# ScalarE takes the input and candidate gates of the next group's first cell ahead of the cell tanh that ends the present group

## The chip, the cores and the metric

One core of one Trainium2 chip runs the whole program. The metric is the device time of the core in microseconds (us), the median of three runs. All data is float32.

## The reference

Four graph layers run one after the other on `x` of shape (32 batches, 256 nodes, 128 features), each with a residual sum and a layer norm behind it. The change lies in the last layer, an LSTM over windows of nodes:

```
for p in range(1, 5):
    nw = 256 // p
    wins = h[:, :nw*p].reshape(B*nw, p, 128)
    # LSTM over the p nodes of each window, zero initial state
    #   i, f, g, o = split(x_t @ Wih.T + h @ Whh.T + bias)
    #   c = sigmoid(f)*c + sigmoid(i)*tanh(g)
    #   h = sigmoid(o)*tanh(c)
    h[:, every p-th node] = last hidden state
x = layernorm(x + h)
```

The first three layers are a gated graph convolution, a graph convolution with batch norms, and graph attention.

## The kernel before

The batches are worked in 8 groups of 4 (`GROUPS`, `GB`). After the first two layers, which run as stages of their own, a software pipeline of slots s = 2 to 10 handles groups at different depths (`slots`): slot s does the attention of group s (flag A, while s < 8), the graph part of the LSTM layer for group s-1 (B), the LSTM cells of group s-2 (L), and the transposes, last norm and output of group s-3 (T). So a slot lasts about as long as the eleven LSTM cells of one group, and the cells of the next group begin where the slot ends.

`STEPS` lists the eleven cells of a group, k = 0 to 10: k = 0 and 1 are the two halves of the p = 1 window (512 columns each, no previous state, so gates I, G, O alone), k = 2 and 3 are p = 2 (512 columns), k = 4 to 6 are p = 3 (340 columns), k = 7 to 10 are p = 4 (256 columns). A cell goes over three engines:

- TensorE: `lstm_x` (L831) multiplies the gate weights with the input into one PSUM bank per gate (`Q[q]`, shown as QQ); `lstm_h` (L843) adds the part with the previous hidden state. One float32 matmul shows as two rows of the trace.
- ScalarE: `lstm_gates` takes the tanh of each gate out of PSUM (L1200, into `TG`, shown as raw). Then `lstm_state` takes the tanh of the cell state (L1236, from `CELL` into `TC`, both shown as raw).
- VectorE: `lstm_cell` (L1680, L1686, L1690) forms `CA = (1+I)*G`, `CF = (1+F)*CELL` and `CELL`; for a first cell one L1680 gives `CELL`. `lstm_state` (L1708) forms the hidden state from `TG[O]` and `TC`, into `HT` or `HS` (shown as HB).

Below, x(k) and h(k) are the two matmul sets of cell k, I(k), G(k), F(k), O(k) its gate tanhs, CELL(k) the VectorE instruction that writes the cell state, TC(k) the tanh of it, and H(k) VectorE's hidden state. Cell 0 after a cell 10 belongs to the next group.

The orders on the engines are written out by hand; each engine runs its own list in order, and semaphores tie the lists together. Around the end of a slot:

- TensorE: h(10) of the present group, the last matmuls of the attention, x(0) of the next group, the transposes of the residual (`a_residual`, L680, only where flag A holds), x(1), the transposes of the group before (`t_turn`, L884), a graph product (`a_spread0`, L786), x(2). x(0) waits only until each bank is read by cell 10's gate tanh; x(1) until it is read by cell 0's. `t_turn` waits for the H(10) of the group that it turns, and x(2) for H(1):

```
            def t_turn(g, par):
                pe.wait_ge(h_ok, NSTEP * (g + 1))
...
                elif s == 0 and p > 1:
                    pe.wait_ge(h_ok, NSTEP * g + LAST_BEFORE[p] + 1)
```

- VectorE: CA(10), CF(10), CELL(10), H(10), the statistics of a norm (`a_stats2`, L1400, where A holds), CELL(0), a residual sum (L1552, where A holds), H(0), CELL(1), six short norm instructions (L1412 to L1422), H(1).
- ScalarE: the gates of cell 10, TC(10), the gates of cell 0, TC(0), the gates of cell 1, TC(1).

In the last two groups (`HALVED`) the cell tanh and the hidden state are made in two halves (L1234 with L1236, L1705 with L1708, VectorE's cells in L1722 to L1738). In the last slot with cells (s = 9) the group is alone: TensorE runs x(0), `t_turn`, x(1), and from k = 2 on the cells run in two lanes (L1219, L865). There `t_turn` turns group 6, whose H(10) ends slot 8.

Of the kernel before, what the change touches and what calls it, by code (L numbers as in the profile page):

```python
# [46 lines left out]
I, F, G, O = range(4)  # L47


def gates_of(k):  # L50

    return [I, G, O] if STEPS[k][1] == 0 else [I, G, F, O]
# [48 lines left out]
def build(nc, x, xt, adj, early_in, later_in, lstm_w, out):  # L101
    ctx = ExitStack()
    with ctx:
# [6 lines left out]
        def reach(eng, s, n):  # L110

            if isinstance(n, int) and n <= 0:
                return
            eng.wait_ge(s, n)
# [182 lines left out]
        def middle(k):  # L297
            return STEPS[k][3] // 2 * GB
# [736 lines left out]
        def _(act):  # L1035

            def norm_apply(k, kk, z, g, to, h=None):
                act.wait_ge(ln[k]["off"], halves(g, h) if k == 1 else g + 1)
                for b in batches(h):
                    for c in range(NC):  # L1040
                        t = 2 * b + c if k == 1 else c * GB + b
                        act.activation(nth(to, t), nth(z, t), ACT.Identity, bias=OFF[kk][:, t:t + 1],  # L1042
                                       scale=RSD[kk][:, t:t + 1]).then_inc(ln[k]["out"], 1)
# [100 lines left out]
            def a_lin(g, some):  # L1144
                f = front(g)
                for b in some:
                    act.wait_ge(wh_ok, 2 * g + b // 2 + 1) if g < 2 else act.wait_ge(s12_ok, g - 1)
                    act.wait_ge(max_ok, TILES * g + 2 * b + 2)
                    reach(act, et_ps, GB * before(g))
                    for c in range(NC):  # L1150
                        t = 2 * b + c
                        s1 = f.WH[:, t, P:P + 1] if g < 2 else S12[:, 0, t:t + 1]
                        e = act.activation(f.E1[:, t], f.MS[:, t], ACT.Prelu, bias=s1, scale=1.0, alpha=SLOPE)
                    e.then_inc(lin_ok, 1)

            def a_exps(g, some):
                f = front(g)
                for b in some:
                    act.wait_ge(eb_ok, 2 * g + b // 2 + 1)
                    act.wait_ge(lin_ok, GB * g + b + 1)  # L1160
                    for c in range(NC):
                        t = 2 * b + c
                        e = act.activation(f.E1[:, t], f.E1[:, t], ACT.Exp, bias=f.EB[:, t:t + 1], scale=1.0,  # L1163
                                           accum_out=DEN[:, t:t + 1] if g > 1 else None)
                    e.then_inc(exps_ok, 1)

            def a_spread(g, h=None):
                act.wait_ge(sp_ps, halves(g, h))
                reach(act, y0_ps, 2 * g)
                act.activation(S0T[:, part(h)], PA[:, part(h)], ACT.Copy).then_inc(sp_ok, size(h))  # L1170

            def a_relu(g, h=None):
                act.wait_ge(y0_ok, halves(g, h))
                act.activation(H0T[:, part(h)], H0T[:, part(h)], ACT.Relu).then_inc(h0_ok, size(h))
# [4 lines left out]
                act.activation(by_batch(HT[:, par])[:, 2 * h:2 * h + 2], PA[:, part(h)].rearrange("p (b n) -> p b n", n=NODES),  # L1179
                               ACT.Relu, scale=2.0).then_inc(h1_ok, 1)  # L1180

            def lstm_gates(g, k):
                p, s, _, nw = STEPS[k]
                n = nw * GB
                j = NSTEP * g + k
                for q in gates_of(k):
                    act.wait_ge(g_ps, NGATE * g + GATE_AT[k, q] + 1)

                    if q == O:
                        reach(act, h_ok, j)  # L1190
                    elif q == F or STEPS[k - 1][1] > 0:
                        reach(act, cf_ok if q == F else ca_ok, FORGETS[NSTEP] * g + FORGETS[k])
                    else:
                        reach(act, cell_ok, j)
                    at = 0
                    if q == F and (g >= HALVED or k == HALF_STEP):
                        at = middle(k)
                        act.activation(TG[q][:, 0:at], Q[q][:, 0:at], ACT.Tanh, scale=0.25,
                                       bias=BL[:, p - 1, q:q + 1]).then_inc(f_half, 1)
                    act.activation(TG[q][:, at:n], Q[q][:, at:n], ACT.Tanh, scale=0.5 if q == G else 0.25,  # L1200
                                   bias=BL[:, p - 1, q:q + 1]).then_inc(g_ok, 1)

            def lane_gates(k, l, some=None):
                p, s, _, nw = STEPS[k]
                v, c = lanes[l], lane_cols(k, l)

                if s == 0 and l == 1 and k > LANED:
                    act.wait_ge(lanes[0].h, lanes[0].step0 + k - LANED)
                for q in some or gates_of(k):
                    act.wait_ge(v.ps, lane_gate(l, k, q))  # L1210
                    if k == LANED:
                        act.wait_ge(h_ok if q == O else cell_ok, NSTEP * LAST + LANED)
                    elif q == O:
                        act.wait_ge(v.h, v.step0 + k - LANED)
                    elif q == F or STEPS[k - 1][1] > 0:
                        reach(act, v.cf if q == F else v.ca, v.forget0 + FORGETS[k])
                    else:
                        act.wait_ge(v.cell, v.step0 + k - LANED)
                    act.activation(TG[q][:, c], v.banks[q][:, c], ACT.Tanh, scale=0.5 if q == G else 0.25,  # L1219
                                   bias=BL[:, p - 1, q:q + 1]).then_inc(v.ok, 1)  # L1220

            def lane_state(k, l):
                v, c = lanes[l], lane_cols(k, l)
                act.wait_ge(v.cell, v.step0 + k - LANED + 1)
                act.activation(TC[:, c], CELL[:, c], ACT.Tanh, scale=0.5).then_inc(v.tc, 1)

            def lstm_state(g, k):
                n = STEPS[k][3] * GB
                j = NSTEP * g + k
                at = 0  # L1230
                if g >= HALVED or k == HALF_STEP:
                    at = middle(k)
                    act.wait_ge(cell_half, halved(g, k)[0])
                    act.activation(TC[:, 0:at], CELL[:, 0:at], ACT.Tanh, scale=0.5).then_inc(tc_half, 1)  # L1234
                act.wait_ge(cell_ok, j + 1)
                act.activation(TC[:, at:n], CELL[:, at:n], ACT.Tanh, scale=0.5).then_inc(tc_ok, 1)  # L1236

            def slot(s, par, A, B, L, T):
                def gates(k):
                    lstm_gates(s - 2, k) if L else None  # L1240

                def state(k):
                    lstm_state(s - 2, k) if L else None

                def cell(k):
                    gates(k)
                    state(k)

                cell(0)
                cell(1)  # L1250
                if s == LAST + 2:
                    for k in range(LANED, NSTEP):

                        first, last = STEPS[k][1] == 0 and k > LANED, k + 1 < NSTEP and STEPS[k + 1][1] == 0
                        lane_gates(k, 0, (O,) if first else None)
                        lane_state(k, 0)
                        lane_gates(k, 1)
                        lane_gates(k + 1, 0, (I, G)) if last else None
                        lane_state(k, 1)
                    return  # L1260
                cell(2)
                a_spread(s - 1, None if A else 0) if B else None
                norm_apply(1, 0, Z, s, X2) if A else None
                cell(3)
                a_spread(s - 1, 1) if B and not A else None
                cell(4)
                a_lin(s, (0,)) if A else None
                gates(5)
                a_relu(s - 1) if B else None
                state(5)  # L1270
                if A:
                    a_lin(s, (1,))
                    a_exps(s, (0,))
                    a_lin(s, (2,))
                gates(6)
                a_lin(s, (3,)) if A else None
                state(6)
                a_exps(s, (1, 2)) if A else None
                gates(7)
                a_exps(s, (3,)) if A else None  # L1280
                state(7)
                cell(8)
                a_mixed(s, (0, 1, 2)) if A else None
                cell(9)
                a_mixed(s, (3,)) if A else None
                cell(10)

            act.wait_ge(bn_ok, HC + 1)
            act.wait_ge(out2_ok, 2 * GROUPS)
# [664 lines left out]
```

## Time and profile before

| | us |
|---|---|
| median of 3 runs | 638.23 |
| lowest, highest | 637.72, 639.11 |
| span of the profiled execution, first to last instruction | 636.4 |
| TensorE matmul rows busy | 621.6 (98%) |
| VectorE busy | 474.8 (75%) |
| ScalarE busy | 433.8 (68%) |
| GpSimd busy | 167.4 (26%) |

The span is what the trace covers; it is 1.8 us below the median of the timed runs, and the profiled execution has no other time. A busy share is an average over stages. Matmuls overlap in the rows: consecutive ones start closer together than one lasts, so whether TensorE is held up is read from the distance of starts, not from the busy share alone. PEld rows are its weight loads.

### The profile page before, as it was taken

Reading aid. Unit: us, or ns where it says so; the run is one execution under the profiler, and the core shown is the slowest. Engines: PE = TensorE matmul, PEld = TensorE weight load, DVE = VectorE, ACT = ScalarE, POOL = GpSimd, SP = SyncE. Lnnn points to the kernel's source line nnn. Section 1 sums busy time; section 2 is a strip of 40 time slices with the busy share of each in tenths; the row PEclk is TensorE's granted clock in tenths of the full one; section 3 lists DMA queues with packets and bytes.
Section 4 is the critical chain, followed back from the end, with each engine's and each line's share of the span. In section 5 each row is a group of like instructions: output and inputs, shape, how many; then the busy total and the mean of one; then the engine's idle time right before and its main releaser. Section 6 shows DMA issues by size and latency. Waiting matters only on the chain.

```text
span 636.4 us, 9580 instructions
## 1 busy us (share of the span) xinstructions
PE 621.6 (98%) x2768; PEld 440.9 (69%) x2768; DVE 474.8 (75%) x1623; ACT 433.8 (68%) x995; POOL 167.4 (26%) x228
## 2 busy tenths in 40 slices
PE   9999999999999999999999999999999999999994
PEld 6756656447975687578658757865885687577794
DVE  4999999876847767866887787688768767465656
ACT  3667767966947766795677577557847766546774
POOL 1464551005233002304503240341143032103211
PEclk9999999999999999999999999999999999999998
DMA  8424000000000000000000000000000000000000
GB/s 337 142 115 166 1 1 1 1 0 2 2 1 1 0 2 0 2 2 33 2 0 2 34 1 2 33 2 1 1 33 2 2 28 6 1 1 33 2 35 33
DMA packets 4372, 16.84 MB, mean 26 GB/s; under 512 B 480, under 2 KB 480, under 8 KB 4192
## 3 DMA queue, kind: packets, MB, share of 16 engines
q1 hardware_dynamic: 4320, 16.23, 6.6%
q8 instruction: 22, 0.36, 0.2%
q14 instruction: 30, 0.25, 0.1%
HBM read 12.03 MB, written 4.19 MB: 26 GB/s over the span
## 4 chain that ended last, share of the span: by engine, by line
PE 76%; DVE 3%; ACT 2%; issue 1%; POOL 0%; POOLq 0%; ACTq 0%; DVEq 0%
PE QQ L831 26%; PE QQ L843 15%; PE PA L814 4%; PE PA L786 4%; PE PB L805 2%; PE PB L796 2%; PE PB L667 2%; PE PA L667 2%; PE PA L767 2%; PE PB L767 2%; PE QQ L865 1%; PE PB L884 1%; PE PB L746 1%; PE PA L746 1%; PE QQ L875 1%
## 5 line engine op out<-in xcount | busy, mean ns | idle before, releaser
L1200 ACT ACTIVATE raw<-QQ,BL 128x256 f32<-128x256 f32 (+2 forms) x279 | 150.1, 558 | 75.1 <-PE QQ L843 37.7
L831 PE MATMUL QQ<-HT,WT 128*128 128x256 f32 (+2 forms) x558 | 183.9, 474 | 1.1 <-ACT raw L1200 0.6
L446 POOL TENSOR_TENSOR RSD<-VAR,pw 128x4 f32<-128x4 f32 (+1 forms) x43 | 61.8, 1438 | 381.7 <-DVE VAR L1422 381.7
L831 PEld LDWEIGHTS QQ<-HT,WT 128*128 128x128 f32 x558 | 103.5, 190 | 59.2 <-issue 28.3
L843 PE MATMUL QQ<-HB,WT 128*128 128x256 f32 (+2 forms) x336 | 100.2, 441 | 0.4 <-DVE HB L1708 0.2
L843 PEld LDWEIGHTS QQ<-HB,WT 128*128 128x128 f32 x336 | 61.2, 190 | 29.3 <-issue 13.4
L1236 ACT ACTIVATE raw<-raw 128x256 f32<-128x256 f32 (+4 forms) x79 | 37.1, 470 | 25.9 <-DVE raw L1690 19.7
L1680 DVE SCALAR_TENSOR_TENSOR raw<-raw 128x256 f32<-128x256 f32 (+2 forms) x60 | 32.5, 542 | 20.2 <-ACT raw L1200 19.6
L1708 DVE SCALAR_TENSOR_TENSOR HB<-raw 128x256 f32<-128x256 f32 (+4 forms) x42 | 20.1, 478 | 23.5 <-ACT raw L1236 23.5
L1042 ACT ACTIVATE X<-Z,OFF,RSD 128x128 f32<-128x128 f32 x80 | 31.8, 482 | 2.0 <-POOL OFF L452 2.0
L512 POOL TENSOR_SCALAR X<-four,MEAN,RSD 128x128 f32<-128x128 f32 x64 | 30.7, 494 | 1.6
L622 PE MATMUL PA<-AHT,X 128*128 128x256 f32 x128 | 29.5, 384 | 1.5 <-ACT X L1042 1.3
L1163 ACT ACTIVATE HB<-HB,EB 128x256 f32<-128x256 f32 x64 | 30.9, 500 | 0.2
L786 PE MATMUL PA<-AD,X 128*128 128x256 f32 x128 | 30.3, 379 | 0.0
L622 PEld LDWEIGHTS PA<-AHT,X 128*128 128x128 f32 x128 | 23.7, 190 | 9.5 <-issue 6.3
L525 POOL TENSOR_SCALAR four<-HB,MEAN,RSD 128x128 f32<-128x128 f32 x56 | 29.7, 544 | 0.7
L636 PE MATMUL QQ<-one_b,later 128*128 128x512 f32 x64 | 29.1, 598 | 0.2 <-ACT one_b L1071 0.2
L814 PE MATMUL PA<-AD,Y 128*128 128x256 f32 x128 | 29.2, 380 | 0.0
L786 PEld LDWEIGHTS PA<-AD,X 128*128 128x128 f32 x128 | 23.9, 191 | 6.8 <-issue 4.1
L814 PEld LDWEIGHTS PA<-AD,Y 128*128 128x128 f32 x128 | 24.2, 190 | 4.2
L1083 ACT ACTIVATE HB<-QQ 128x512 f32<-128x512 f32 x32 | 17.9, 586 | 12.8 <-PE QQ L636 12.5
L599 PE MATMUL PB<-four,AD 128*128 128x512 f32 x56 | 25.7, 601 | 0.4 <-DMA four<-in_x 0.4
(249 smaller groups left out, 1177.5 us busy)
## 6 DMA issues: line engine op xcount, KB each, us to landing
four<-in_x SPq DMA_DIRECT2D x8, 512.0 KB, 4.0
raw<-in_xt SPq DMA_DIRECT2D x8, 512.0 KB, 6.5
out<-four SPq DMA_DIRECT2D x7, 512.0 KB, 2.6
WT<-in_lstm SPq DMA_DIRECT2D x1, 2048.0 KB, 8.0
later<-in_later SPq DMA_DIRECT2D x1, 725.5 KB, 10.3
AD<-in_adj SPq DMA_DIRECT2D x2, 256.0 KB, 4.8
out<-four SPq DMA_DIRECT2D x2, 256.0 KB, 2.0
early<-in_early SPq DMA_DIRECT2D x1, 275.0 KB, 4.5
```

The lines of the kernel that those rows point to most:

```text
L446: pool.tensor_tensor(RSD[kk][:, ts], VAR[kk][:, ts], pw[:, ts], ALU.pow).then_inc(ln[k]["rstd"], some)
L512: pool.tensor_scalar(tile_of(X1, g, c, b), nth(f.Z2, t), MEAN[f.kk2][:, t:t + 1], RSD[f.kk2][:, t:t + 1], ALU.add, ALU.mult).then_inc(ln[2 ...
L622: mm = pe.matmul(PA[:, b * NODES:(b + 1) * NODES], tile_of(X1, g, m, b), AHT[:, m, :], start=(m == 0), stop=(m == NC - 1))
L786: mm = pe.matmul(PA[:, b * NODES:(b + 1) * NODES], tile_of(X1, g, m, b), ADJT[:, m, :], start=(m == 0), stop=(m == NC - 1))
L814: mm = pe.matmul(PA[:, b * NODES:(b + 1) * NODES], turned(Y, m, b), ADJT[:, m, :], start=(m == 0), stop=(m == NC - 1))
L831: mm = pe.matmul(steps_view(Q[q], k), WT[:, 0, (p - 1) * 4 + q, :], ht_view(par, k), start=True, stop=(s == 0))
L843: pe.matmul(Q[q][:, 0:nw * GB], WT[:, 1, (p - 1) * 4 + q, :], HS[:, (k - 1) % 2, 0:nw * GB], start=False, stop=True).then_inc(g_ps, 1)
L1042: act.activation(nth(to, t), nth(z, t), ACT.Identity, bias=OFF[kk][:, t:t + 1], scale=RSD[kk][:, t:t + 1]).then_inc(ln[k]["out"], 1)
L1163: e = act.activation(f.E1[:, t], f.E1[:, t], ACT.Exp, bias=f.EB[:, t:t + 1], scale=1.0, accum_out=DEN[:, t:t + 1] if g > 1 else None)
L1200: act.activation(TG[q][:, at:n], Q[q][:, at:n], ACT.Tanh, scale=0.5 if q == G else 0.25, bias=BL[:, p - 1, q:q + 1]).then_inc(g_ok, 1)
L1236: act.activation(TC[:, at:n], CELL[:, at:n], ACT.Tanh, scale=0.5).then_inc(tc_ok, 1)
L1680: dve.scalar_tensor_tensor(out=target[:, 0:n], in0=TG[I][:, 0:n], scalar=1.0, in1=TG[G][:, 0:n], op0=ALU.add, op1=ALU.mult).then_inc(cell_ ...
```

## The change

`lstm_gates` gets a list of gates. At the end of a slot, ScalarE now takes I(0) and G(0) of the next group between the gates of cell 10 and TC(10); at the start of the next slot only O(0) is left, ahead of TC(0). The first slot with cells (s = 2) still does all three gates there. The hand-over happens at the ends of slots 2 to 8, seven times; no instruction is added or taken away, and no semaphore or wait of an instruction is altered.

```
-            def lstm_gates(g, k):
+            def lstm_gates(g, k, some=None):
...
-                for q in gates_of(k):
+                for q in some or gates_of(k):
...
-                cell(0)
+                if not L:
+                    return
+                lstm_gates(s - 2, 0, None if s == 2 else (O,))
+                state(0)
                 cell(1)
...
-                cell(10)
+                gates(10)
+                lstm_gates(s - 1, 0, (I, G))
+                state(10)
```

This is ScalarE's list at the end of slot 2, where the slots 3 to 7 end alike. The first two rows are F(10) and O(10), the row that moves is TC(10), the pair of 512 columns is I(0) and G(0) of the next group, and the last two rows are O(0) and TC(0).

```order
 L1200 ACTIVATE raw<-QQ,BL 128x256 [waits cf_ok,g_ps]
 L1200 ACTIVATE raw<-QQ,BL 128x256 [waits h_ok,g_ps]
-L1236 ACTIVATE raw<-raw 128x256 [waits cell_ok]
 L1200 ACTIVATE raw<-QQ,BL 128x512 [waits ca_ok,g_ps] x2
+L1236 ACTIVATE raw<-raw 128x256 [waits cell_ok]
 L1200 ACTIVATE raw<-QQ,BL 128x512 [waits h_ok,g_ps]
 L1236 ACTIVATE raw<-raw 128x512 [waits cell_ok]
```

TC(10) now stands behind two gate tanhs that wait for TensorE (g_ps) and for CA(10) (ca_ok).

This is ScalarE's list at the end of slot 8, where TC(10) comes in two halves (L1234 and L1236 of 128 columns).

```order
 L1200 ACTIVATE raw<-QQ,BL 128x128
 L1200 ACTIVATE raw<-QQ,BL 128x256 [waits h_ok,g_ps]
+L1200 ACTIVATE raw<-QQ,BL 128x512 [waits ca_ok,g_ps] x2
 L1234 ACTIVATE raw<-raw 128x128 [waits cell_half]
 L1236 ACTIVATE raw<-raw 128x128 [waits cell_ok]
-L1200 ACTIVATE raw<-QQ,BL 128x512 [waits ca_ok,g_ps] x2
 L1200 ACTIVATE raw<-QQ,BL 128x512 [waits h_ok,g_ps]
 L1234 ACTIVATE raw<-raw 128x256 [waits cell_half]
```

Both halves of TC(10) now stand behind I(0) and G(0). The lists of TensorE, VectorE, GpSimd and SyncE keep their order.

## Rows read from the trace of the kernel before

**Rows 1.** The page of the profiled execution: its head and the engines' busy times.

```profile
span 636.4 us, 9580 instructions
...
PE 621.6 (98%) x2768; PEld 440.9 (69%) x2768; DVE 474.8 (75%) x1623; ACT 433.8 (68%) x995; POOL 167.4 (26%) x228
```

**Rows 2.** Timeline, end of slot 2 (start us, us, engine, line, instruction, [idle before <-releaser]).

```profile
245.19 2.74 PE L831 MATMUL QQ<-HT,WT 128*128 128x512 f32 x6
...
245.92 0.45 DVE L1680 SCALAR_TENSOR_TENSOR raw<-raw 128x256 f32<-128x256 f32 x1
...
247.50 0.42 ACT L1236 ACTIVATE raw<-raw 128x256 f32<-128x256 f32 x1 [2.08 <-DVE raw L1690]
...
247.82 1.82 ACT L1200 ACTIVATE raw<-QQ,BL 128x512 f32<-128x512 f32 x3
```

**Rows 3.** Timeline, start of slot 3, from H(10) to the weight load of x(2).

```profile
248.02 0.42 DVE L1708 SCALAR_TENSOR_TENSOR HT<-raw 128x256 f32<-128x256 f32 x1 [0.55 <-ACT raw L1236]
248.36 0.86 DVE L1400 BATCH_NORM_STATS2 STL<-four 128x6 f32<-128x128 f32 x4
249.14 0.67 DVE L1680 SCALAR_TENSOR_TENSOR raw<-raw 128x512 f32<-128x512 f32 x1
...
249.85 0.63 ACT L1236 ACTIVATE raw<-raw 128x512 f32<-128x512 f32 x1 [0.20 <-DVE raw L1680]
250.39 1.94 ACT L1200 ACTIVATE raw<-QQ,BL 128x512 f32<-128x512 f32 x3
...
251.67 0.69 DVE L1680 SCALAR_TENSOR_TENSOR raw<-raw 128x512 f32<-128x512 f32 x1
...
252.39 0.63 ACT L1236 ACTIVATE raw<-raw 128x512 f32<-128x512 f32 x1
...
253.12 0.69 DVE L1708 SCALAR_TENSOR_TENSOR HT<-raw 128x512 f32<-128x512 f32 x1
...
253.87 0.30 PEld L831 LDWEIGHTS QQ<-HT,WT 128*128 128x128 f32 x2 [0.21 <-DVE HT L1708]
```

**Rows 4.** The same weight load of x(2) at the start of slot 7.

```profile
483.86 0.30 PEld L831 LDWEIGHTS QQ<-HT,WT 128*128 128x128 f32 x2 [0.20 <-DVE HT L1708]
```

**Rows 5.** Timeline of TensorE, single matmul rows: fourth of x(0), first and second of x(2).

```profile
246.48 0.59 PE L831 MATMUL QQ<-HT,WT 128*128 128x512 f32 x1
...
253.91 0.67 PE L831 MATMUL QQ<-HT,WT 128*128 128x512 f32 x1
...
254.41 0.59 PE L831 MATMUL QQ<-HT,WT 128*128 128x512 f32 x1
```

**Rows 6.** Timeline of ScalarE: a gate that TensorE released, and a cell tanh behind a gate.

```profile
255.04 0.69 ACT L1200 ACTIVATE raw<-QQ,BL 128x512 f32<-128x512 f32 x1 [2.01 <-PE QQ L831]
...
544.17 0.69 ACT L1200 ACTIVATE raw<-QQ,BL 128x512 f32<-128x512 f32 x1 [0.17 <-PE QQ L831]
544.76 0.41 ACT L1234 ACTIVATE raw<-raw 128x256 f32<-128x256 f32 x1
```

**Rows 7.** Timeline, start of slot 8: x(1), the second half of H(1), first row of x(2).

```profile
536.04 2.84 PE L831 MATMUL QQ<-HT,WT 128*128 128x512 f32 x6 [0.62 <-ACT raw L1200]
...
540.78 0.42 DVE L1708 SCALAR_TENSOR_TENSOR HT<-raw 128x256 f32<-128x256 f32 x1
...
541.40 0.59 PE L831 MATMUL QQ<-HT,WT 128*128 128x512 f32 x1
```

**Rows 8.** Timeline, end of slot 8: TC(10), fourth row of x(0), H(10), first transposes of `t_turn`.

```profile
585.08 0.31 ACT L1234 ACTIVATE raw<-raw 128x128 f32<-128x128 f32 x1 [0.21 <-DVE raw L1738]
...
585.40 0.59 PE L831 MATMUL QQ<-HT,WT 128*128 128x512 f32 x1
...
585.71 0.28 DVE L1708 SCALAR_TENSOR_TENSOR HT<-raw 128x128 f32<-128x128 f32 x1
...
586.69 1.11 PE L884 MATMUL PB<-ident,HT 128*128 128x128 f32 x8
```

## The prediction, made before the changed kernel ran

> **What bounds the kernel now.** I read the page first, then the timeline at the slot ends, then single rows there. On the page TensorE's matmul rows cover 98% of the span, every other engine at most 75% [rows 1]. That share could hide waits, so I looked at distances of starts. In x(0) six rows of 512 columns last 2.74 us together and 0.59 us each, so they start (2.74 - 0.59) / 5 = 0.43 us apart [rows 2, 5], and this distance hardly varies over the long middle of a slot: TensorE streams without a break and its order is the time. A change on ScalarE can then matter only where TensorE waits for something that ScalarE made. The places to look at are the few instructions of TensorE behind a slot end that wait on the cells: x(1), `t_turn` and x(2).
>
> **Where the end of a slot is tight.** ScalarE stands idle 2.08 us ahead of TC(10), which starts at 247.50 when CELL(10) is done [rows 2]. That is the hole into which the two gates go. What follows TC(10) is one closed chain [rows 3]: H(10) at 248.02, the norm statistics at 248.36, CELL(0) at 249.14 (VectorE goes straight from one to the other), TC(0) at 249.85 (released by CELL(0)), the gates of cell 1 at 250.39 right behind it, CELL(1) at 251.67, TC(1) at 252.39, H(1) at 253.12 to 253.81, and the weight load of x(2) at 253.87, which had stood 0.21 us for H(1). The matmul rows tell how much of this TensorE feels: the first row of x(2) starts at 253.91 and the second at 254.41, 0.50 apart where 0.43 is usual [rows 5], so some 0.07 us are lost already and there is no slack left. The same load waits 0.20 us in slot 7 [rows 4], and the slots 3 to 7, five of them, repeat this to 0.02 us. Whatever delays TC(10) here therefore delays TensorE.
>
> **What the change moves, and the cost of each part.** No instruction, DMA or wait comes or goes; the two gate tanhs do not get cheaper, they only stand elsewhere.
>
> I(0) finds its inputs ready inside the hole: CA(10), which must have read the old gate, ends at 245.92 + 0.45 = 246.37 [rows 2], so I(0) runs from about 246.4 and costs nothing; CELL(10), the work that hides it, is busy until 247.50.
>
> G(0) is the one that does not fit. It needs the second matmul of x(0), whose last row, the fourth of six, starts at 246.48 and lasts 0.59 [rows 5]. A gate that stands waiting starts 0.04 us behind the end of such a row (254.41 + 0.59 = 255.00, gate at 255.04) [rows 5, 6]. So G(0) starts at 247.11, 0.39 us before TC(10) would. A cell tanh behind a gate of 512 columns starts 0.59 us after the gate (544.17 to 544.76) [rows 6]. TC(10) then starts at 247.70, late by **0.20 us**. Bounds from the nearest rows: a gate behind a 512-column tanh started 0.54 after it (249.85 to 250.39) [rows 3], and a gate lasts 0.69 in all [rows 6]; these give 0.15 and 0.30. I take 0.20, since its row is of the same pair of instructions.
>
> By the Trainium skill, ScalarE: Activation LUTs (What ACT_TABLE_LOAD costs), an ACTIVATE with a pointer bias takes 280 ns plus 0.833 ns a column and neighbours overlap by 93 ns; my estimate from that is 0.61 us from start to start at 512 columns. The row shows 0.59. By the page the delay would be 0.22 us and the whole sum larger by some 0.1 us; the measured row is used.
>
> *Slots 3 to 7.* The chain of [rows 3] hangs together without a gap, so H(1) and x(2) come 0.20 us later each time; the gates done early do not shorten it, because CELL(0) stood behind VectorE's own statistics and I(1) behind TC(0), not behind G(0). 5 x 0.20 = **1.00 us** (0.75 to 1.50).
>
> *Slot 8.* Here there are no residual transposes between x(0) and x(1), and x(1) waits 0.62 us for I(0) [rows 7]. That wait goes: I(0) is now done before x(0) ends. But what is late next is x(2). Its H(1) ends at 540.78 + 0.42 = 541.20, hidden so far behind the graph product that TensorE runs ahead of x(2), and x(2) starts at 541.40. Delayed by the same 0.20 it ends at 541.40; TensorE starts 0.10 behind such an end (253.81 to 253.91) and loses 0.07 at the restart [rows 3, 5]. So x(2) starts about 541.50 and loses **0.17 us** (0.12 to 0.27) against before, however early TensorE arrives.
>
> *Slot 9.* At the end of slot 8 there is no hole: x(0) starts right behind cell 10 and TC(10)'s first half follows its gates by 0.21 us, at 585.08 [rows 8]. G(0) is released at 585.40 + 0.59 + 0.04 = 586.03, and TC(10) starts 0.59 later, at 586.62: late by 1.54 us. H(10)'s second half, ended at 585.99 before, ends at 587.53. `t_turn` stands on TensorE directly behind x(0), needs this H(10), and started at 586.69. It will start at about 587.63, and with the restart the stall is 0.94 + 0.07 = **1.01 us** (0.9 to 1.2). Behind it in TensorE's order is x(1), and everything of the last group hangs on that, so I see nothing that gives it back.
>
> Sum: 1.00 + 0.17 + 1.01 = 2.18 us. On the profiled span that is 636.4 to 638.6. The median of the runs stands 1.8 us above that span, and I add the sum to it: 638.23 + 2.18 = **640.4 us**, 0.34% more. With the bounds above the case runs from 1.8 to 3.0 us, so 640.0 to 641.2.
>
> **The rivals.**
> *Only slot 9 pays.* If x(2) is not really held by H(1) in slots 3 to 8, because the load's wait of 0.21 us is covered by the product still streaming, the 0.20 us vanish and 1.0 us is left: 639.2 us. For it: just 0.07 us of that wait shows in the matmul rows. Against it: a wait that already shows cannot absorb more. 12%.
>
> *Slot 9 is covered.* If the last group's lanes wait further on for something that does not hang on `t_turn` or x(1), the 1.01 us come back and 1.17 are left: 639.4 us. For it: the tail has other short waits. Against it: I found none whose releaser does not follow from x(1). 8%.
>
> *Faster.* ScalarE's gates are what holds the next group back: with two of them gone, the wait of 0.62 us at x(1) in slot 8 and the five of 0.07 at x(2) fall away and TensorE streams on: 0.62 + 5 x 0.07 = 0.97 us less, 637.3. It needs G(0) to be released by 247.50 - 0.59 = 246.91 or earlier, where the rows say 247.11, and H(1) ahead of its old time; slot 9's loss must fail too. The Trainium skill, Perfetto Trace Analysis (Identifying the Most-Contended Engine), would have TensorE judged by its weight-load share, not its matmul share; that share is 69% here, and by this rule TensorE would have room and such an earlier release would pay. Starts 0.43 us apart where a pair of loads takes 0.30 [rows 3] say that the loads' share is low because the matmuls are long, not because TensorE idles. 5%.
>
> **How the numbers follow.** The forecast has 75%. A change below 0.2% (1.28 us) is about what a measurement of this kernel cannot tell from none; by that the first two rivals end within it, if closely, and the forecast beyond it but for its lowest edge. Slower 0.76, same 0.18, faster 0.06. The range 639.1 to 641.2 takes in the forecast's bounds and reaches down to the two milder cases; the faster one and the tails stay out.
>
> **What would show it.** In the changed profile: I(0) at about 1.1 us before TC(10)'s old place and G(0) 0.59 us before TC(10); TC(10) behind the gate, no longer released by CELL(10), in all seven hand-overs; the step from the fourth row of x(0) to TC(10) 1.22 us; from TC(10) to x(2) as long as before. The 0.62 us wait of x(1) for ScalarE gone, x(2) of slots 3 to 8 waiting for H(1) longer by 0.2 (in slot 8 by about 0.9, since TensorE gets there sooner), and a new wait of `t_turn` for VectorE's H(10) of 0.8 to 0.9 us in slot 9. It is wrong if the distance from H(10) to x(2) shrinks, or if the last group's end does not move with `t_turn`.

## The result, and the profile after

| | before | after |
|---|---|---|
| median of 4 runs, in alternation on one chip | 638.12 us (637.72 to 639.11) | 640.41 us (640.16 to 641.06) |
| span of the profiled execution | 636.4 us | 638.8 us |

The ratio is 1.004, with a 95% interval of 1.0028 to 1.0052: the change costs 2.29 us by the medians, 0.4%, and the interval lies wholly above 1. In the head of the page after, answering [rows 1], nothing stands out:

```profile
span 638.8 us, 9580 instructions
...
PE 623.3 (98%) x2768; PEld 441.0 (69%) x2768; DVE 473.6 (74%) x1623; ACT 435.6 (68%) x995; POOL 169.7 (27%) x228
```

All counts of instructions are those of before, and the granted clock of TensorE stands at nine tenths or more in nearly every slice of both pages, so the time is not the clock's. It must lie in waits, and the place is found by laying the two traces on each other. The kernel issues the same matmuls in the same order, so the same row can be looked up in both and the starts subtracted. These are four rows of TensorE's timeline of before: x(0) of slot 8, x(0) and x(1) of slot 9, and one of the last rows of the program. (For x(0) of slot 3 it is 245.19 in [rows 2].)

```profile
532.68 1.46 PE L831 MATMUL QQ<-HT,WT 128*128 128x512 f32 x3
...
584.12 0.59 PE L831 MATMUL QQ<-HT,WT 128*128 128x512 f32 x1
...
587.64 1.02 PE L831 MATMUL QQ<-HT,WT 128*128 128x512 f32 x2
...
626.26 0.41 PE L892 MATMUL QQ<-ident,HT 128*128 128x128 f32 x2
```

After, the same rows (the first one is x(0) of slot 3):

```profile
245.53 2.74 PE L831 MATMUL QQ<-HT,WT 128*128 128x512 f32 x6
...
533.99 5.40 PE L831 MATMUL QQ<-HT,WT 128*128 128x512 f32 x12
...
585.56 2.74 PE L831 MATMUL QQ<-HT,WT 128*128 128x512 f32 x6
...
590.08 2.31 PE L831 MATMUL QQ<-HT,WT 128*128 128x512 f32 x5
...
628.66 0.40 PE L892 MATMUL QQ<-ident,HT 128*128 128x128 f32 x2
```

The shifts are 0.34, 1.31, 1.44, 2.44 and 2.40 us. So five slots (3 to 7) cost 0.97, slot 8 costs 0.13, slot 9 costs 1.00 at once and keeps 0.96 to the end. The 0.34 is there before the change does anything: 0.26 of it stands at the first product that waits for its input (L599, at 5.84 us where before has 5.58), the rest gathers in small waits up to 155 us, and two executions of the unchanged program differ by 0.46 at the same place (below). The change itself is worth 2.40 - 0.34 = 2.06 us in the trace.

**Slots 3 to 7.** Timeline of after, end of slot 2 and start of slot 3, answering [rows 2, 3]. VectorE's lines stand 5 higher than before (H at L1713, was L1708):

```profile
246.77 1.37 ACT L1200 ACTIVATE raw<-QQ,BL 128x512 f32<-128x512 f32 x2 [1.01 <-DVE raw L1685]
...
247.12 0.43 DVE L1695 SCALAR_TENSOR_TENSOR raw<-raw 128x256 f32<-128x256 f32 x1
...
248.04 0.41 ACT L1236 ACTIVATE raw<-raw 128x256 f32<-128x256 f32 x1
...
248.55 0.43 DVE L1713 SCALAR_TENSOR_TENSOR HT<-raw 128x256 f32<-128x256 f32 x1 [1.01 <-ACT raw L1236]
248.89 0.87 DVE L1405 BATCH_NORM_STATS2 STL<-four 128x6 f32<-128x128 f32 x4
...
249.67 0.68 DVE L1685 SCALAR_TENSOR_TENSOR raw<-raw 128x512 f32<-128x512 f32 x1
...
250.39 0.63 ACT L1236 ACTIVATE raw<-raw 128x512 f32<-128x512 f32 x1 [0.63 <-DVE raw L1685]
...
252.20 0.69 DVE L1685 SCALAR_TENSOR_TENSOR raw<-raw 128x512 f32<-128x512 f32 x1
...
254.41 0.30 PEld L831 LDWEIGHTS QQ<-HT,WT 128*128 128x128 f32 x2 [0.40 <-DVE HT L1713]
```

I(0) and G(0) are the two gates at 246.77. TC(10), at 248.04, no longer has a releaser: it stands directly behind the gates, though CELL(10) (L1695) ended at 247.55. The chain from there to the load of x(2) is as long as before, 254.41 - 248.04 = 6.37 us against 253.87 - 247.50 = 6.37 in [rows 2, 3], and the load waits 0.40 where it waited 0.21. ScalarE waits 0.63 for CELL(0) where the gates used to be (250.39): the room that the move made is idle.

**Slot 8**, timeline of after, answering [rows 7]: the second half of H(1), then the load and the first rows of x(2):

```profile
542.27 0.42 DVE L1713 SCALAR_TENSOR_TENSOR HT<-raw 128x256 f32<-128x256 f32 x1
...
542.75 0.30 PEld L831 LDWEIGHTS QQ<-HT,WT 128*128 128x128 f32 x2 [1.08 <-DVE HT L1713]
542.75 1.13 PE L831 MATMUL QQ<-HT,WT 128*128 128x512 f32 x2 [0.68 <-DVE HT L1713]
```

x(0) and x(1) run as twelve rows with no wait of TensorE between them (533.99 above; only the last row starts 0.09 late), the wait of 0.62 for I(0) is gone, and TensorE stands 0.68 in front of x(2) instead.

**Slot 9**, timeline of after, answering [rows 8]: G(0) (the second gate), TC(10)'s first half, H(10)'s second half, `t_turn`:

```profile
587.48 0.69 ACT L1200 ACTIVATE raw<-QQ,BL 128x512 f32<-128x512 f32 x1 [0.17 <-PE QQ L831]
588.07 0.30 ACT L1234 ACTIVATE raw<-raw 128x128 f32<-128x128 f32 x1
...
588.68 0.28 DVE L1713 SCALAR_TENSOR_TENSOR HT<-raw 128x128 f32<-128x128 f32 x1
...
589.02 1.23 PE L884 MATMUL PB<-ident,HT 128*128 128x128 f32 x8 [0.72 <-DVE HT L1713]
```

G(0) waits for TensorE, TC(10) follows it by 0.59, and `t_turn` has a wait of 0.72 us that no row of before has.

### The profile page after: what moved, and what is told of

It reads as the page before. It is cut to its first block, busy times and chain, and to the rows that moved or that the text cites. A ratio compares the mean times of both kernels' runs of the same rounds, so it can differ in the third digit from the quotient of the medians.

```text
span 638.8 us, 9580 instructions
## 1 busy us (share of the span) xinstructions
PE 623.3 (98%) x2768; PEld 441.0 (69%) x2768; DVE 473.6 (74%) x1623; ACT 435.6 (68%) x995; POOL 169.7 (27%) x228
## 4 chain that ended last, share of the span: by engine, by line
PE 76%; DVE 3%; ACT 3%; issue 1%; POOL 0%; POOLq 0%; ACTq 0%; DVEq 0%
PE QQ L831 26%; PE QQ L843 15%; PE PA L814 4%; PE PA L786 4%; PE PB L805 2%; PE PB L796 2%; PE PB L667 2%; PE PA L667 2%; PE PA L767 2%; PE PB L767 2%; PE QQ L865 1%; PE PB L746 1%; PE PA L746 1%; PE PB L884 1%; PE QQ L875 1%
## 5 line engine op out<-in xcount | busy, mean ns | idle before, releaser
L1200 ACT ACTIVATE raw<-QQ,BL 128x256 f32<-128x256 f32 (+2 forms) x279 | 151.8, 559 | 85.8 <-PE QQ L843 37.5
L1236 ACT ACTIVATE raw<-raw 128x256 f32<-128x256 f32 (+4 forms) x79 | 37.1, 469 | 15.6 <-DVE raw L1685 7.8
L1713 DVE SCALAR_TENSOR_TENSOR HB<-raw 128x256 f32<-128x256 f32 (+4 forms) x42 | 20.1, 479 | 23.5 <-ACT raw L1236 23.5
L512 POOL TENSOR_SCALAR X<-four,MEAN,RSD 128x128 f32<-128x128 f32 x64 | 32.7, 526 | 1.6
L1713 DVE SCALAR_TENSOR_TENSOR HT<-raw 128x256 f32<-128x256 f32 (+4 forms) x37 | 19.1, 517 | 11.0 <-ACT raw L1236 10.9
```

The lines of the kernel that those rows point to most:

```text
L512: pool.tensor_scalar(tile_of(X1, g, c, b), nth(f.Z2, t), MEAN[f.kk2][:, t:t + 1], RSD[f.kk2][:, t:t + 1], ALU.add, ALU.mult).then_inc(ln[2 ...
L1713: dve.scalar_tensor_tensor(out=to[:, at:nw], in0=steps_view(TG[O], k)[:, at:nw], scalar=1.0, in1=steps_view(TC, k)[:, at:nw], op0=ALU.add, ...
```

## The experiments

"Step" below is the shift of a TensorE row against before, gained within a stretch, as worked out above: from x(0) of slot 3 to that of slot 8, on to that of slot 9, and on to the last row of the program. It is taken from starts to the nanosecond, so the last digit can differ by 0.02 from the rounded rows. Medians of the experiments are of 8 to 11 runs of the kernel and 21 to 31 of before, each pair on one chip; experiments 1 to 4 ran on one chip, 5 to 8 on another, 9 and 10 on a third.

| kernel | start | slots 3–7 | slot 8 | slot 9 | steps of slots 3–9 | median / before, us | ratio [95%] |
|---|---|---|---|---|---|---|---|
| after (4 runs each) | 0.35 | +0.96 | +0.14 | +0.95 | +2.04 | 640.41 / 638.12 | 1.004 [1.0028, 1.0052] |
| 1 I(0) alone moved | 0.05 | −0.38 | −0.31 | +0.11 | −0.58 | 637.86 / 638.02 | 0.9999 [0.999, 1.0008] |
| 2 moved in slots 2–7 | 0.35 | +0.98 | +0.14 | −0.07 | +1.05 | 639.61 / 638.02 | 1.0027 [1.0017, 1.0037] |
| 3 moved in slot 8 | 0.60 | −0.36 | −0.28 | +0.93 | +0.29 | 638.83 / 638.02 | 1.0013 [1.0005, 1.0022] |
| 4 as 2, statistics behind H(0) | 0.87 | +0.04 | −0.31 | +0.04 | −0.23 | 638.54 / 638.02 | 1.0006 [0.9998, 1.0015] |
| 5 after, `t_turn` behind x(1) | 0.69 | +0.92 | +0.13 | +0.15 | +1.20 | 640.04 / 638.26 | 1.0026 [1.0016, 1.0037] |
| 6 before, `t_turn` behind x(1) | 0.34 | −0.06 | −0.01 | −0.34 | −0.41 | 638.23 / 638.26 | 0.9999 [0.999, 1.0008] |
| 7 as 4, `t_turn` behind x(1) | 0.06 | 0.00 | −0.31 | −0.35 | −0.66 | 637.74 / 638.26 | 0.999 [0.9981, 0.9999] |
| 8 before, unaltered | 0.46 | −0.06 | −0.01 | −0.11 | −0.17 | 638.25 / 638.26 | 1.0001 [0.9992, 1.001] |
| 9 as 7, I(0) alone moved | 2.49 | −0.14 | −0.77 | −0.34 | −1.25 | 637.43 / 638.11 | 0.999 [0.9981, 0.9999] |
| 10 as 9, statistics in place | 0.71 | −0.30 | −0.32 | −0.35 | −0.97 | 637.37 / 638.11 | 0.9991 [0.9982, 1.0] |

The column "start" belongs to no edit: experiment 8 is before once more and has 0.46. Part of it is TensorE's clock. By the traces' record it is granted at its upper level (2.4 GHz) from 4.61 us on in before, from 6.45 in experiment 8 and from 9.90 in experiment 9: during the first products of 128 columns, during the first of 512, and during the fifth of 512. Until then rows start twice as far apart (products of 512 columns in experiment 9: 0.86 us, where 0.43 is usual). The profiled execution of experiment 9 was also the slowest of its eleven runs, 639.45 us. The steps come from one profiled execution each, and experiment 8 shows that their sum repeats to 0.17 us. The medians follow the steps only roughly: of two versions whose steps lie half a microsecond apart the medians need not tell which is ahead, and experiment 4 lies 0.75 us above its steps.

**1. Only I(0) moved.** It tells whether the price is G(0)'s alone.

```diff
-                lstm_gates(s - 2, 0, None if s == 2 else (O,))
+                lstm_gates(s - 2, 0, None if s == 2 else (G, O))
...
-                lstm_gates(s - 1, 0, (I, G))
+                lstm_gates(s - 1, 0, (I,))
```

> I(0) alone goes ahead of TC(10), in all seven hand-overs; G(0) and O(0) stay behind it. Theory A (G(0), released late by TensorE, pushes TC(10)): TC(10) of slots 2 to 7 starts when CELL(10) is done, as before, so slots 3 to 8 cost nothing, although the wait of x(1) for I(0) in slot 8 (0.62 us) is gone. In slot 8's end I(0) is released at 585.18 in the old clock and TC(10) follows 0.59 later, 0.69 late; t_turn then starts only about 0.1 late. Sum against before: +0.15 us (0 to 0.4). Theory B (each gate that moves costs its share, whichever it is): about half of the 2.2 us, +1.1. Theory C (the gates of cell 0 hold the next group back, and the harm comes from slot 9): -0.6 or better.

Timeline of experiment 1, end of slot 2 (I(0), TC(10)) and slot 9 (TC(10)'s first half, `t_turn`):

```profile
246.47 0.69 ACT L1200 ACTIVATE raw<-QQ,BL 128x512 f32<-128x512 f32 x1 [1.01 <-DVE raw L1685]
...
247.28 0.42 ACT L1236 ACTIVATE raw<-raw 128x256 f32<-128x256 f32 x1
...
585.12 0.30 ACT L1234 ACTIVATE raw<-raw 128x128 f32<-128x128 f32 x1
...
586.07 1.23 PE L884 MATMUL PB<-ident,HT 128*128 128x128 f32 x8
```

I(0) ends at 247.16 and TC(10) starts when CELL(10) is done. `t_turn` shows no wait. The steps of after (+0.96, +0.14, +0.95) are gone but for 0.11, and the median is that of before: I(0) is free at the ends of slots 2 to 7, and G(0) pays it all there. At the end of slot 8 I(0) makes TC(10) late too (585.12; 0.68 later than before, with the shift of slot 9's x(0), −0.64, taken out), and `t_turn` pays a restart, its eight rows lasting 1.23 us for 1.11 [rows 8]: that is the +0.11, which the expectation had as 0.1. The theory that each gate costs its share is out. The −0.38 and −0.31 that stand in place of the first two steps are not I(0)'s gain: experiment 3 has −0.36 and −0.28 in the same slots, where it changes nothing. With them the sum of the steps, −0.58, falls below the 0 to 0.4 expected.

**2 and 3. The two places apart:** the move in slots 2 to 7 only, and in slot 8 only.

```diff
+                lstm_gates(s - 2, 0, None if s in (2, LAST + 2) else (O,))
+                lstm_gates(s - 1, 0, (I, G)) if s <= LAST else None
...
+                lstm_gates(s - 2, 0, (O,) if s == LAST + 2 else None)
+                lstm_gates(s - 1, 0, (I, G)) if s == LAST + 1 else None
```

> The change at the ends of slots 2 to 7 only; the end of slot 8 and slot 9 as before. Theory A: 0.19 us at each of five hand-overs and 0.15 at the sixth, +1.1 us against before (0.8 to 1.4). Rival 'only slot 9 pays': 0. Theory C: below 0, by the wait of 0.62 us at x(1) in slot 8.

> The change at the end of slot 8 only; the other six hand-overs as before. Theory A: t_turn waits for H(10) and all behind it is late: +1.0 us against before (0.85 to 1.15). Rival 'slot 9 is covered': 0. With the run that leaves slot 8 out, the two sums should give the whole change, 2.1 to 2.2 us.

Experiment 2 keeps +0.98 and +0.14 and loses slot 9's step; experiment 3 keeps +0.93 in slot 9 alone. So the two parts are independent and add up: 1.05 + 0.93 = 1.98 against the 2.04 of after. By the medians they are +1.59 and +0.81, together 2.40; experiment 2 came out above the 0.8 to 1.4 expected, with an interval that reaches from 1.1 to 2.4 us, and what its runs have beyond the steps stays open. Experiment 3's median lies just below the 0.85 to 1.15 expected. It brought a surprise: slots 3 to 8, where its code is that of before, ran 0.64 us faster. That is taken up at the end.

**4. Statistics out of the chain.** If VectorE's norm statistics hold CELL(0), then moving them behind it should take away the price of slots 3 to 7 while G(0) still stands ahead of TC(10). To experiment 2 it adds, on VectorE:

```diff
                 state(0)
+                a_stats2(s - 1, 1) if B and s > 2 else None
                 inner(1)
...
                 cell(10)
-                a_stats2(s, 1) if A else None
```

> The change at the ends of slots 2 to 7, and VectorE takes the four norm statistics of the slot before behind H(0) of the next slot instead of ahead of CELL(0). Theory A holds that the early gates bring nothing because CELL(0) stands behind these statistics: without them CELL(0) follows H(10) at once, 0.6 us earlier than before, since G(0) is done. In slots 3 to 7 the residual sum then bounds CELL(1) and the gain at x(2) is at most 0.07 each; in slot 8, without a residual sum, H(1) comes about 0.5 us earlier and x(2) with it. Sum against before: -0.5 us (-0.9 to 0). If the statistics were not the cause (the chain bound by ScalarE's order alone), it stays at the +1.1 us of the run without this edit.

Timeline of experiment 4, start of slot 3: x(0), TC(10), TC(0), I(1) and G(1), the statistics, CELL(1), TC(1), the load of x(2):

```profile
246.06 2.74 PE L831 MATMUL QQ<-HT,WT 128*128 128x512 f32 x6
...
248.56 0.41 ACT L1236 ACTIVATE raw<-raw 128x256 f32<-128x256 f32 x1
...
250.18 0.62 ACT L1236 ACTIVATE raw<-raw 128x512 f32<-128x512 f32 x1
...
250.70 1.41 ACT L1200 ACTIVATE raw<-QQ,BL 128x512 f32<-128x512 f32 x2
...
251.75 0.87 DVE L1405 BATCH_NORM_STATS2 STL<-four 128x6 f32<-128x128 f32 x4
...
252.53 0.68 DVE L1685 SCALAR_TENSOR_TENSOR raw<-raw 128x512 f32<-128x512 f32 x1
...
253.24 0.63 ACT L1236 ACTIVATE raw<-raw 128x512 f32<-128x512 f32 x1 [0.27 <-DVE raw L1685]
...
254.72 0.30 PEld L831 LDWEIGHTS QQ<-HT,WT 128*128 128x128 f32 x2 [0.20 <-DVE HT L1713]
```

TC(10) is as late as in after, but TC(0) comes 250.18 - 246.06 = 4.12 us behind x(0), where after has 4.86 and before 4.66. So the statistics were what carried the delay on, and the price of slots 3 to 7 falls from +0.98 to +0.04 (slot 4 has +0.11, the others −0.03 to −0.01). The gain that I had expected beyond that does not come, since of those 0.54 us against before nearly all is lost on the way to TC(1): 7.18 us behind x(0), before 7.20. The statistics now delay CELL(1) instead of CELL(0): G(1) ends at 250.70 + 1.41 = 252.11, and CELL(1) starts at 252.53, right behind them. The median is +0.52 where −0.5 was expected, so the expectation missed by 1 us; the interval holds no change. No run moves the statistics alone. In before that could have brought CELL(0) forward by less than 0.1 us, an estimate: it started at 249.14 [rows 3], and G(0), the second of the gates at 247.82 [rows 2], ended at 249.07.

**5 and 6. `t_turn` behind x(1).** In slot 9 `t_turn` goes behind x(1) on TensorE, and `t_sum` behind cell 1 on VectorE, once in after (5) and once in before (6):

```diff
                     lstm_x(LAST, par, 0)
-                    t_turn(s - 3, 1 - par)
                     lstm_x(LAST, par, 1)
+                    t_turn(s - 3, 1 - par)
...
                     cell(0)
-                    t_sum(s - 3)
                     cell(1)
+                    t_sum(s - 3)
```

> The whole change, with one order altered in slot 9: TensorE runs x(1) ahead of t_turn, and VectorE takes the residual sum that reads the turned tiles behind CELL(1) and H(1) instead of ahead of CELL(1). Theory A (slot 9's 1.0 us is TensorE standing in t_turn for H(10), with x(1) queued behind it): x(1) no longer waits for H(10), and the loss of slot 9 falls from 1.0 us to between -0.3 and +0.2; against before +0.8 to +1.3 is left, from slots 3 to 8. If instead the late chain H(10), CELL(0), TC(0) itself carries the loss, it stays at +2.2 us.

> The kernel before with the same altered order in slot 9 and no gate moved: the control for the run with the whole change. x(1) starts 0.95 us sooner, and I(1) follows TC(0), some 0.5 us sooner than before: -0.3 to -0.6 us against before, unless VectorE's later residual sum holds up the lanes by as much (0).

Timeline of experiment 5, slot 9 (x(0) and x(1), TC(10), `t_turn`, and the first product of cell 2's second lane, L865, which waits for H(1)):

```profile
585.86 5.36 PE L831 MATMUL QQ<-HT,WT 128*128 128x512 f32 x12
...
588.36 0.30 ACT L1234 ACTIVATE raw<-raw 128x128 f32<-128x128 f32 x1
...
591.05 1.12 PE L884 MATMUL PB<-ident,HT 128*128 128x128 f32 x8
...
593.62 0.70 PE L865 MATMUL PA<-HT,WT 128*128 128x256 f32 x2 [0.16 <-DVE HT L1713]
```

Experiment 6, the same product, behind an x(0) at 584.39:

```profile
591.80 0.59 PE L865 MATMUL PA<-HT,WT 128*128 128x256 f32 x2
```

TC(10) is as late as before the edit, 588.36 - 585.86 = 2.50 us behind x(0) (after: 588.07 - 585.56 = 2.51), but TensorE has twelve rows to run meanwhile and `t_turn` does not wait. Slot 9's step falls from +0.95 to +0.15. But the same edit without the gates (6) gives −0.34 there, so under this order the two gates still cost 0.15 + 0.34 = 0.49, against 0.95 under the old one: the place of `t_turn` behind H(10) makes half of the 1 us. The other half is the late chain H(10), CELL(0), TC(0), up to H(1), which TensorE meets at cell 2 instead: 593.62 - 585.86 = 7.76 us behind x(0) and with a wait, where experiment 6 has 591.80 - 584.39 = 7.41 and none, and the restart adds to it. The expectation of experiment 5 had set these two theories against each other; each holds in part. Its median, +1.78, lies above the 0.8 to 1.3 expected, its steps, +1.20, within. In experiment 6 the median does not change.

**7, 9 and 10. The parts together:** experiment 4 with 5's edit (7); the same with I(0) alone moved (9); and that with the statistics in their old place (10). Experiment **8** is before, unaltered, and tells how well the steps repeat.

> Both altered orders together, the statistics behind H(0) and t_turn behind x(1), with the two gates moved at the ends of slots 2 to 7 only. If the parts add up: slots 3 to 7 at 0, slot 8 at -0.3 as in the run with the statistics alone, slot 9 as in the control without the change, -0.3 to -0.6; the sum -0.5 to -0.9 us from slot 2 on, on top of the start of the program, which differed by 0 to 0.9 us between the profiles so far.

> The kernel before, unaltered, as a run of its own: 0 against before. In the profile before, GpSimd's third scaling (L512) starts just ahead of CA(10), and CF(10) and CELL(10) take 0.58 and 0.49 us; in all profiles since, it starts at the same time, takes 1.0 us, and VectorE's two take 0.42 and 0.43, with CELL(10) 0.27 us earlier. If that follows the program, this run shows the slow pair again and TC(10) 2.31 us behind x(0); if it differs between executions, TC(10) comes 2.04 us behind x(0), as in the hand-overs left alone in the run with the change at slot 8 only.

> Only I(0) ahead of TC(10), at the ends of slots 2 to 7, with the statistics behind H(0) and t_turn behind x(1). Theory A: TC(10) is not pushed, CELL(0) follows H(10) and G(0) without the statistics between, so H(1) is early enough in slots 3 to 7 (0 to -0.08 each) and in slot 8 the whole wait of x(1), 0.8 us, stays gained; slot 9 -0.35 as in the control. Sum of the steps from slot 2 on -1.2 to -1.6 us against before; in the median, with the scatter of the program's start, -0.7 to -2.

> The same with the statistics left ahead of CELL(0). Slots 3 to 7 0 to -0.08 each, slot 8 -0.3 as in the run with I(0) alone, slot 9 -0.35: steps of -0.65 to -1.1 us. The difference between the two runs is what the statistics hold back in slot 8, some 0.5 us.

Timeline of experiment 9, slot 8: x(0) from its second row on and x(1), the statistics, the second half of H(1), the load of x(2):

```profile
535.46 4.88 PE L831 MATMUL QQ<-HT,WT 128*128 128x512 f32 x11
...
539.88 0.87 DVE L1405 BATCH_NORM_STATS2 STL<-four 128x6 f32<-128x128 f32 x4
...
542.41 0.42 DVE L1713 SCALAR_TENSOR_TENSOR HT<-raw 128x256 f32<-128x256 f32 x1
...
542.88 0.30 PEld L831 LDWEIGHTS QQ<-HT,WT 128*128 128x128 f32 x2 [0.25 <-DVE HT L1713]
```

In slot 8 the load's wait is down from the 1.08 of after to 0.25, and the step is −0.77. Experiment 10, which differs from it by the statistics alone, has −0.32 there, and experiment 3 has −0.28 without an edit. So I(0) by itself brings next to nothing, and I(0) with the statistics out of the chain brings some 0.45 us; what the statistics alone would bring no run shows. Steps of −0.66, −1.25 and −0.97, within what was expected of each, became −0.52, −0.68 and −0.74 in the medians, of which that of experiment 9 falls just short of the −0.7 to −2 expected. Versions 7 and 9 lie ahead of before by 0.1% with an interval that ends just below 1, and version 10 touches 1. All three beat the changed kernel by some 3 us. Of version 10's steps the −0.62 of slots 3 to 8 is what experiment 3 has there without an edit (−0.64), and the −0.35 of slot 9 is that of experiment 6 without any gate moved; so its lead is not to be credited to I(0).

## Why the prediction held

It was 640.4 us, the median 640.41. That it agrees to 0.01 us is luck: the trace gives 2.06 us where 2.18 was summed, the medians differ by 2.29, and a program's start alone scatters by some tenths. The terms of the sum are what held.

*I(0) is free.* Right for the ends of slots 2 to 7, of which it was said; shown by experiment 1 against experiment 3, which has the same steps there without it.

*TC(10) is late by 0.20, because G(0) needs the second matmul of x(0).* Right. From the fourth row of x(0) (three distances of 0.43 behind 245.53) to TC(10) it is 248.04 - 246.82 = 1.22 us, as forecast, and 248.04 - 0.34 - 247.50 = 0.20.

*The chain hands this on whole, five times.* Right: 6.37 us from TC(10) to x(2) in both kernels, five slots 0.96 to 0.97 for 1.00. That VectorE's statistics are the link that ties CELL(0) to H(10) was argued; experiment 4 shows it. In all five slots the step arises at the first two rows of x(2), as the sum had it (by the starts in the two traces). This also puts away the rival in which slot 9 alone pays: the load's wait of 0.21 us had no slack in it.

*Slot 8, 0.17.* Measured 0.13 to 0.14: H(1) came 0.18 later against x(0) (542.27 - 533.99 and 540.78 - 532.68), TensorE started 0.06 behind its end, not 0.10, and the restart cost 0.10 instead of 0.07. The wait there is 0.68, not "about 0.9". The wait removed at x(1) bought nothing, because x(2) stood behind the delayed H(1): the gain was turned into a new wait.

*Slot 9, 1.01.* TC(10) late by 588.07 - 1.44 - 585.08 = 1.55 (1.54 forecast), `t_turn` by 589.02 - 1.44 - 586.69 = 0.89 (0.94), the restart 0.11 (0.07): 1.00 at x(1), and 0.96 at the end. The wait is 0.72, below the 0.8 to 0.9 named, since it is counted from the end of x(0)'s last row, and in before `t_turn` had started 0.16 ahead of that end (586.69 against 586.26 + 0.59 = 586.85). The rival in which slot 9 is covered falls: +0.93 in experiment 3, which moves nothing else, and of the 1.00 no more than 0.04 came back, where experiment 8 has −0.11 in slot 9 without an edit. What the prediction left out is that the late chain costs by another way too: take `t_turn` from behind it, and 0.49 remains (experiments 5 and 6). In the changed kernel this second price is hidden by the stand at `t_turn`: the lane's product waits 0.47 us for H(1) there as in before.

*The rival "faster".* It needed G(0) ready by 246.91; it was ready at 247.11. Nor would an earlier matmul have been enough. I(0) is itself released only at 246.77 - 0.34 = 246.43 in the time of before, a gate follows a gate by (1.82 - 0.69) / 2 = 0.57 [rows 2] and TC(10) a gate by 0.59, so by this estimate TC(10) would start at 247.59 and still be 0.09 late. Even the sound half of this rival, I(0), which is ready in time and does remove slot 8's wait, bought nothing when moved alone: slot 8's step is −0.31 in experiment 1 and −0.28 in experiment 3, where that slot has the order of before. H(1) sets the start of x(2) there in any case.

*A cell tanh behind a gate.* The distance of 0.59 us that the sum used was met again (587.48 to 588.07). The estimate of 0.61 from the Trainium skill, ScalarE: Activation LUTs (What ACT_TABLE_LOAD costs), was 0.02 off, which would have made 0.1 us in the sum.

## What to carry to other kernels

An engine's idle hole can be filled only by work whose inputs are there before the hole ends: here the hole was 2.08 us, the work 1.4 us, and still the second piece started 0.39 us before the old end, because a matmul set its start; the first piece, too, was released only when half of the hole had passed. Look up when each moved instruction is *released*, not whether it fits, and move only those that are released early. Then follow the instruction that was passed (here the tanh and its H) to the next place where the bounding engine reads it: a delay of 0.20 us cost its full size there, and 1.5 us cost 1.0. Where the bounding engine has independent work, putting that ahead of the reader (as x(1) ahead of `t_turn`) took away half of the price; the rest came back at the next reader of the same chain. Run such an edit on the old kernel too: without experiment 6, experiment 5 would have read as nearly all of it.

## What the runs showed of the hardware that was not expected

The length of cell 10's three VectorE instructions, CA(10), CF(10) and CELL(10), has two outcomes, and a few nanoseconds in their start go with them. The three run while GpSimd scales a 128x128 tile (L512). Experiment 8, the kernel before once more, shows both outcomes in one execution: at the end of slot 2 and at the end of slot 6. Its timeline, GpSimd's scaling, the second and third VectorE instruction and TC(10), each time:

```profile
246.35 0.71 POOL L512 TENSOR_SCALAR X<-four,MEAN,RSD 128x128 f32<-128x128 f32 x1
...
246.75 0.59 DVE L1686 SCALAR_TENSOR_TENSOR raw<-raw 128x256 f32<-128x256 f32 x1
...
247.44 0.49 DVE L1690 SCALAR_TENSOR_TENSOR raw<-raw 128x256 f32<-128x256 f32 x1
...
247.97 0.42 ACT L1236 ACTIVATE raw<-raw 128x256 f32<-128x256 f32 x1 [2.09 <-DVE raw L1690]
...
476.38 1.00 POOL L512 TENSOR_SCALAR X<-four,MEAN,RSD 128x128 f32<-128x128 f32 x1
...
476.72 0.42 DVE L1686 SCALAR_TENSOR_TENSOR raw<-raw 128x256 f32<-128x256 f32 x1
...
477.24 0.42 DVE L1690 SCALAR_TENSOR_TENSOR raw<-raw 128x256 f32<-128x256 f32 x1
...
477.70 0.42 ACT L1236 ACTIVATE raw<-raw 128x256 f32<-128x256 f32 x1 [1.81 <-DVE raw L1690]
```

Where VectorE's first instruction starts 0.02 us behind the scaling (246.37), the later two take 0.59 and 0.49 and the scaling 0.71; where it starts 0.01 behind (476.39), they take 0.42 each and the scaling 1.00. TC(10) comes 2.33 us behind x(0) in the first case (x(0) at 245.64) and 2.04 in the second (475.66). The twelve traces have 72 such hand-overs, at the ends of slots 2 to 7. In 41 of them the outcome is the quick one, with VectorE's first -1 to 16 ns behind the scaling; in 31 it is the slow one, 16 to 31 ns behind. Before has the slow one six times (scaling at 245.89, VectorE at 245.92 [rows 2], 0.71 us long), after and experiments 1 to 4 have the quick one throughout. The row of after, end of slot 2:

```profile
246.25 1.00 POOL L512 TENSOR_SCALAR X<-four,MEAN,RSD 128x128 f32<-128x128 f32 x1
```

VectorE's first starts at 246.26 there. The outcome does not follow from the moved gates: experiments 5 and 7 have them and are slow throughout, experiments 6 and 8 are slow but for the end of slot 6, and experiments 9 and 10 have both. What sets the start on either side stays open.

What it is worth shows within one execution. In experiment 8 slot 7, behind the one quick hand-over, has a step of −0.09, slots 3 to 6 of 0.01 each; in experiment 10 slot 6, behind the one slow hand-over, has +0.01, the other four of slots 3 to 7 have −0.07 to −0.09. In slot 8 it is −0.28 to −0.32 behind a quick hand-over (experiments 1, 3 and 10) and −0.01 behind a slow one (6 and 8). This accounts for the 0.64 us of experiment 3 in slots that its edit leaves alone, and for the like steps of experiments 1 and 10. That GpSimd's start is the cause of the outcome is not shown, since no run changed it alone.

It also means that a part of cell 10 that had seemed fixed in [rows 2] was 0.27 us longer than it must be. With G(0) ahead of TC(10) that saving is hidden: experiment 5, slow, has +0.92 and +0.13 in slots 3 to 7 and 8, after, quick, +0.96 and +0.14. So against a kernel of the old order with the quick outcome, as in experiment 3, the change would cost 0.96 + 0.36 = 1.32 us in slots 3 to 7 and 0.14 + 0.28 = 0.42 in slot 8, together 0.64 more than against the kernel before as profiled.

The Trainium skill, SBUF — State Buffer (SBUF: two separate sides), says that a VectorE instruction with two inputs from SBUF and a GpSimd instruction that reads SBUF share a pair of ports as an exclusive lock: whichever starts first has it for the whole instruction, and the other fully blocks. That the two lengthen each other agrees with the runs. That the first to start wins does not show in them: by the recorded starts the scaling is first in both cases above, and in the second it is the scaling that is drawn out, from the 0.45 us of one with no such VectorE instruction beside it to 1.00.
